# Layer 1's mixture of experts: every expert for every token, or the two chosen ones from a sorted list

## The chip, the cores and the metric

The kernel runs on one NeuronCore of a Trainium2 chip. The core has a matrix engine (TensorE, PE in the profile), a vector engine (VectorE, DVE), an activation engine (ScalarE, ACT), GpSimd (POOL) and a queue engine that issues transfers (SyncE, SP). PE writes its results to PSUM, eight banks of 128 partitions; the other data lie in SBUF or in DRAM. The metric is the device time of one execution in microseconds; lower is better. Float32 is used everywhere but in the attention scores, whose operands are split into bfloat16 parts.

## The reference

Four sequences of 1,024 tokens with 128 features (4,096 tokens, 32 tiles of 128) pass two layers. Each layer normalises x to xn, takes an attention s of xn and a gate g = silu(ffn(xn)), and returns x + s*g. In layer 1 the ffn is a mixture of eight experts with two chosen per token:

```python
logits = einsum('th,eh->te', x, router_w)
topk_logits, topk_idx = top_k(logits, 2)
probs = softmax(topk_logits)
combine = zeros((T, E)).at[arange(T)[:, None], topk_idx].add(probs)
hmid = gelu(einsum('th,efh->etf', x, w1) + b1[:, None, :])      # F = 256
y = einsum('etf,ehf->eth', hmid, w2) + b2[:, None, :]
out = einsum('eth,te->th', y, combine)
```

Written so, all eight experts are computed for every token and six of the eight results are multiplied by zero. Layer 1's attention is causal and differential, with 8 pairs of heads.

## The kernel before

The program has four blocks, one after the other, each with its own instruction lists for the five engines: the token stage of layer 0, its attention stage, the token stage of layer 1 and its attention stage.

**The token stage** (`token_stage(layer, ...)`) goes over 8 groups of 512 tokens. `steps` interleaves three things in the order of the expert number k = 0..7: the experts of group g (`body("expert")`), the front of group g+1 (transposes, router logits, projections q, k, v, the choice of experts, the split of q and k into three bfloat16 parts), and the statistics and normalisation of group g+2. In layer 1 `hidden` does two matmuls of 512 columns per expert (L866), ACT applies gelu with the bias (L800), eight matmuls of 128 columns give the expert's result (L898; each float32 matmul stands in the trace as two), and DVE adds it, weighted by the column C of the routing matrix, to the accumulator ACC (L1084). The bias b2 comes in by a small matmul of C (L940). ACT and DVE turn ACC into G, half of the silu by tanh, and SP stores it in `g_dram` (L750).

The split of q and k: DVE clamps them into FQ (L983), ACT rounds to PARTS (L831), GpSimd forms the rest (L682), ACT rounds that (L847), GpSimd forms the third part (L685). SP stores each group with one issue for v (L728), six for q (L736) and three for k (L745). PARTS has two buffers.

**The attention stage** (`attention_stage`) goes over 32 units of 128 queries. Its order on each engine is fixed ahead by `attention_plan`, which places tasks by costs and aims (`COST`, `AIM`). The tasks of a unit that matter here: GpSimd splits the row maxima (`msplit`, L1321 to L1327) and SP copies them in six small transfers next to the queries (L1266), on which PE's exponent scores wait; PE turns the output back (`oback`), DVE divides (`onorm`), GpSimd finds the root mean square by Newton steps (`orms`, L1331 to L1334), PE turns and projects (`oturn` L1467, `oproj` L1470), DVE multiplies by the gate (`final`, L1564), GpSimd adds x (L1341) and SP stores. After that addition GpSimd loads x and g for the unit two further on (`load_xg`, L1303 and L1304).

x of layer 1's first groups is loaded near the end of the attention stage of layer 0, into the buffer KR that layer 1 does not need (`X1`, `XN1`), and DVE normalises the first group there, in the task `final` of the last unit (L512).

## Time and profile before

| What | Value |
|---|---|
| Time, median of 3 runs | 1991.66 us (1989.51 to 1996.56) |
| Span of the profiled execution, whose page gives no other time | 1994.7 us |
| PE busy | 1724.8 us, 86% of the span |
| DVE / ACT / POOL busy | 1335.0 / 1194.0 / 1128.4 us |
| Instructions | 78,600 |

The busy time is that of the whole span; the four blocks differ, so the table by stretch in the rows below says more. The profiled span lies 3.0 us above the median of the runs and inside their range.

### The profile page before, as it was taken

How to read it: one execution, taken by the hardware profiler on the slowest of the kernel's cores; microseconds unless marked ns; L12 is line 12 of the kernel's file. 1: busy time of each engine (PE TensorE's matmuls, PEld its weight loads, DVE VectorE, ACT ScalarE, POOL GpSimd, SP SyncE). 2: the span in 40 equal slices, each digit the busy share in tenths (PEclk: the TensorE clock that was granted, in tenths of full speed). 3: DMA queues.
4: the chain of work that ended last, by engine and by line, in shares of the span. 5: the costliest groups of instructions: out<-in, count | busy, mean ns of one | idle time of the engine just before them, and what ended most of it. 6: DMA issues, size and time to landing. Idle time of an engine off the chain costs nothing. (4 is left out here: it accounts for less than half of the span.)

```text
span 1994.7 us, 78600 instructions
## 1 busy us (share of the span) xinstructions
PE 1724.8 (86%) x34080; PEld 1310.1 (66%) x34080; DVE 1335.0 (67%) x1975; ACT 1194.0 (60%) x1438; POOL 1128.4 (57%) x1489
## 2 busy tenths in 40 slices
PE   6887789999999989999988689999967878788886
PEld 4666678777787777778766566667635555555554
DVE  5552777777777758877776244544477888777882
ACT  2333477777787768777876534444425656566565
POOL 4755589987899769987995522221012333334333
PEclk9988799999998999999998789999958999999898
DMA  3476032222322222222112122133112112121100
GB/s 111 124 212 173 24 96 76 76 71 76 88 69 80 62 76 83 86 70 70 48 59 69 58 68 82 58 91 97 54 26 50 31 49 48 37 59 31 26 24 17
DMA packets 166301, 139.91 MB, mean 70 GB/s; under 512 B 91715, under 2 KB 157014, under 8 KB 160454
## 3 DMA queue, kind: packets, MB, share of 16 engines
q1 hardware_dynamic: 150966, 100.40, 17.2%
q10 hardware_dynamic: 9616, 21.89, 4.5%
q0 software_dynamic: 5376, 12.59, 2.2%
q8 instruction: 271, 4.44, 0.9%
q14 instruction: 72, 0.59, 0.1%
HBM read 90.91 MB, written 43.12 MB: 67 GB/s over the span
## 5 line engine op out<-in xcount | busy, mean ns | idle before, releaser
L1364 ACT ACTIVATE a_EX<-bank 128x1024 f32<-128x1024 f32 x624 | 615.4, 1026 | 288.9 <-PE bank L1236 235.0
L1490 DVE TENSOR_TENSOR a_PM<-bank,a_PM 128x1024 f32<-128x1024 f32 x336 | 401.7, 1221 | 129.2 <-PE bank L1236 118.0
L1316 POOL TENSOR_TENSOR a_SN<-a_SN,a_MB 128x1024 f32<-128x1024 f32 x176 | 421.0, 2429 | 48.0 <-DMA a_MB<-m_dram 47.2
L1513 DVE TENSOR_REDUCE a_M<-bank 128x2 f32<-128x1024 f32 (+3 forms) x304 | 339.0, 1163 | 82.0 <-PE bank L1249 53.3
L1453 PE MATMUL bank<-a_EX,VV 128*32 128x128 f32 x9984 | 359.7, 288 | 6.5 <-issue 4.9
L1236 PE MATMUL bank<-QS,KS 51*128 51x128 bf16 (+1 forms) x4992 | 234.9, 228 | 93.9 <-DMA QS<-a_MP 29.9
L1453 PEld LDWEIGHTS bank<-a_EX,VV 128*32 128x32 f32 x9984 | 269.8, 114 | 51.0 <-issue 22.7
L1236 PEld LDWEIGHTS bank<-QS,KS 51*128 51x128 bf16 (+1 forms) x4992 | 156.7, 99 | 185.8 <-issue 52.0
L1360 ACT ACTIVATE a_SN<-bank 128x1024 f32<-128x1024 f32 x176 | 176.7, 1024 | 57.6 <-PE bank L1215 56.3
L1368 ACT ACTIVATE a_SN<-a_SN 128x1024 f32<-128x1024 f32 x176 | 184.9, 1060 | 34.7 <-POOL a_SN L1316 34.7
L1215 PE MATMUL bank<-QP,rel_t 112*128 112x32 bf16 x5632 | 197.9, 177 | 3.0 <-issue 2.7
L1215 PEld LDWEIGHTS bank<-QP,rel_t 112*128 112x128 bf16 x5632 | 170.3, 96 | 4.0 <-issue 3.9
L1084 DVE SCALAR_TENSOR_TENSOR t_ACC<-bank,t_C,t_ACC 128x128 f32<-128x128 f32 x256 | 72.0, 344 | 145.9 <-PE bank L898 144.7
L898 PEld LDWEIGHTS bank<-t_w,t_HM 128*128 128x128 f32 x1024 | 123.8, 194 | 49.2 <-ACT t_HM L800 31.3
L1236 PE MATMUL bank<-QS,KR 48*128 48x128 bf16 (+1 forms) x2688 | 124.0, 224 | 29.9 <-DVE a_PM L1490 12.8
L1210 PE MATMUL bank<-QN,KS 112*128 112x64 bf16 x2816 | 141.5, 193 | 8.6 <-PEq L671 7.6
L1249 PE MATMUL bank<-KS,QS 48*128 48x128 bf16 (+3 forms) x1152 | 117.8, 293 | 28.6 <-DVE a_M L1513 14.7
L898 PE MATMUL bank<-t_w,t_HM 128*128 128x128 f32 x1024 | 128.8, 280 | 10.9 <-ACT t_HM L800 9.5
L529 POOL COPY QP<-QS 48x1024 bf16<-48x1024 bf16 x64 | 138.1, 2157 | 0.0
L1236 PEld LDWEIGHTS bank<-QS,KR 48*128 48x128 bf16 (+1 forms) x2688 | 79.4, 97 | 75.1 <-issue 28.9
L866 PE MATMUL bank<-t_XT,t_w 128*128 128x512 f32 x256 | 124.3, 609 | 0.0
L1497 DVE TENSOR_TENSOR a_PM<-a_SN 128x1024 f32<-128x1024 f32 x64 | 97.8, 1527 | 33.5 <-ACT a_SN L1360 27.6
(163 smaller groups left out, 2410.2 us busy)
## 6 DMA issues: line engine op xcount, KB each, us to landing
a_MB<-m_dram SPq DMA_DIRECT2D x32, 1024.0 KB, 5.0
QS<-q_dram SPq DMA_DIRECT2D x192, 96.0 KB, 2.9
KS<-k_dram ACTq DMA_DIRECT2D x16, 768.0 KB
q_dram<-t_PARTS SPq DMA_DIRECT2D x32, 192.0 KB, 2.8
k_dram<-t_PARTS SPq DMA_DIRECT2D x16, 384.0 KB, 2.9
QS<-a_MP SPq DMA_DIRECT2D x384, 2.0 KB
KR<-kr_dram ACTq DMA_DIRECT2D x8, 576.0 KB
q_dram<-t_PARTS SPq DMA_DIRECT2D x32, 128.0 KB, 2.6
```

Of the source, the lines that this page charges most:

```text
L529: last = pool.tensor_copy(QP[rows, r, :, :, a], QS[rows, q, :, :, :].rearrange("k p h (q b) -> k q (p h) b", b=2)[:, :, :, a])
L898: last = pe.matmul(y, HM[:, k % 2, h, t * P:(t + 1) * P], w2[:, k, h, :], start=h == 0, stop=h == 1)
L1210: pe.matmul(out_b[:, :, 4 * pair:4 * pair + 4], KS[0:KD, it.u // NB % 2, pair, it.jb * P:(it.jb + 1) * P], QN[:, r, pair, q0:q0 + CQ // 2, ...
L1215: last = pe.matmul(out_b[:, i, :], rel_t[:, y:y + P], QP[:, r, q0 + i, :, :].rearrange("k h a -> k (h a)"), start=False, stop=i == CQ // 2 ...
L1236: last = pe.matmul(bank[:, 2 * it.n + hh, k * P:(k + 1) * P], kblock(hh, rows, it.u, it.jb, pair), QS[hh * HALF:hh * HALF + rows, it.u % Q ...
L1316: pool.tensor_tensor(near_view(sn), near_view(sn), as_near(MB[:, :, :], it.part), ALU.add)\
L1360: act.activation(near_buffer(u, jb)[:, part, :], src.rearrange("p b c -> p (b c)"), ACT.Copy).then_inc(act_done, 1)
L1364: act.activation(as_banks(EX[:, it.need % ER[layer]], part), by_head, ACT.Exp, scale=SCALE).then_inc(act_done, 1)
L1368: act.activation(sn, sn, ACT.Exp, scale=SCALE).then_inc(nexp_done, 1)
L1453: last = pe.matmul(dst_o, VV[:, u // NB % 2, jb, vo:vo + 32], ex, start=bool(it.first) and h < 4, stop=bool(it.last), skip_group_check=True)
L1490: dve.tensor_tensor(pm, mb.rearrange("p hh (k i) -> p hh k i", k=4), pm, ALU.max).then_inc(max_used, 1)
L1513: dve.tensor_reduce(target.rearrange("p (hh k) -> p hh k", hh=2)[:, :, p0:p0 + g], mb[:, :, 0:g * width].rearrange("p hh (k j) -> p hh k j ...
```

## The change

Layer 1's token stage becomes a function of its own, `routed_stage`, with two halves (chunks) of 16 tiles, 4 groups each. Each half is normalised whole and its logits are taken first. `route` picks two experts per token and works out, with three matmuls and some small DVE operations, a place for each (token, choice) pair in a list sorted by expert, each expert's part padded to tiles of 128: 39 tiles ("steps") per half. GpSimd scatters the normalised rows to these places in DRAM (`xs_dram`) by 32 indirect transfers per half. The list is read back in quads of four steps, turned by PE, run through the step's expert, whose number is read into a register of each engine, and stored in `y_dram`. The q, k and v work of a half comes after its routing; all of it comes before the first step. The third part of the split moves from GpSimd to DVE.

The gate is no longer stored. In layer 1's attention stage GpSimd gathers, per unit, the two result rows of each token by indirect transfers, weights and adds them (`mix`), ACT takes a tanh, and GpSimd forms twice the silu (`gate`). The plan's costs and order are as before. In layer 0's attention stage SP also writes zeros over both lists (26 transfers of 192 KB), and the first half's x, not its first group, is loaded, measured and normalised near the end. Unchanged: layer 0's token stage, the attention of both layers.

```diff
+CHUNKS = 2
+CT = T // P // CHUNKS
+CG = GROUPS // CHUNKS
+STEPS = (2 * CT * P + E * (P - 1)) // P
+QUADS = -(-STEPS // 4)
+XGR = 4
...
+        def routed_stage(stage):
...
+            FQ = local("FQ", [P, 2, 2, GROUP])
+            FR = local("FR", [P, 2, 2, GROUP])
+            PARTS = local("PARTS", [P, 2, 3, 2, GROUP], BF16)
...
+            W = local("W", [P, 4, FF])
+            XS = local("XS", [P, 3, 4, P])
+            XST = local("XST", [P, 2, 4, P])
+            HM = local("HM", [P, 3, 2, P])
+            Y = local("Y", [P, 3, 4, P])
...
+                def _(pool):
+                    pool.memset(VA[:, :, :, :, VD:VD + 1], 1.0).then_inc(v_ones, 1)
+                    pool.wait_ge(zeroed, 16 * (CHUNKS * STEPS // 3))
+                    for c in range(CHUNKS):
+                        pool.wait_ge(slots_ready, c + 1)
+                        for t in range(CT):
+                            for k in range(2):
+                                at = SLOT[:, k, c * CT + t:c * CT + t + 1]
+                                pool.indirect_dma_start(out=xs_dram[c], out_offset=bass.IndirectOffsetOnAxis(ap=at, axis=0),
+                                                        in_=X1[c][:, t, :], in_offset=None).then_inc(scattered[c], 16)
...
+                    def load_slots(q):
+                        c, i = divmod(q, QUADS)
+                        sp.wait_ge(scattered[c], 16 * 2 * CT)
+                        if q >= 3:
+                            sp.wait_ge(xs_psum, q - 2)
+                        size = quad_size(q)
+                        sp.dma_start(XS[:, q % 3, 0:size, :], xs_dram[c].rearrange("(s p) d -> p s d", p=P)[:, 4 * i:4 * i + size, :])\
+                          .then_inc(xs_in[q % 3], 16)
+
+                    def store_y(q):
+                        c, i = divmod(q, QUADS)
+                        size = quad_size(q)
+                        sp.wait_ge(y_ready, steps_before(q) + size)
+                        sp.dma_start(y_dram[c].rearrange("(s p) d -> p s d", p=P)[:, 4 * i:4 * i + size, :], Y[:, q % 3, 0:size, :])\
+                          .then_inc(y_out[q % 3], 16)
...
+                    for f in range(GROUPS):
+                        store_v(f)
+                        store_qk(f)
+                        if f == 5:
+                            for q in range(3):
+                                load_slots(q)
+                    for u in range(QR):
+                        load_q(1, sp, u)
+                    for q in range(CHUNKS * QUADS):
+                        store_y(q)
+                        if q + 3 < CHUNKS * QUADS:
+                            load_slots(q + 3)
...
+                    def first_part(f):
+                        if f >= 2:
+                            act.wait_ge(qk_stored[f % 2], QKS * (f // 2))
+                        act.wait_ge(qk_taken, 2 * f + 2)
+                        act.activation(PARTS[:, f % 2, 0, :, :], FQ[:, f % 2, :, :], ACT.Copy).then_inc(p1_ready, 1)
...
+                    for f in range(CG, GROUPS):
+                        values(f)
+                        first_part(f)
+                        if f > CG:
+                            second_part(f - 1)
+                    second_part(GROUPS - 1)
...
+                    turn_slots(0)
+                    for c in range(CHUNKS):
+                        pe.wait_ge(steps_ready, c + 1)
+                        for i in range(QUADS):
+                            q = c * QUADS + i
+                            if q + 1 < CHUNKS * QUADS:
+                                turn_slots(q + 1)
+                            for k, e in enumerate(experts_of(mybir.EngineType.PE, c, i)):
+                                s = step_index(c, 4 * i + k)
+                                hidden(q, k, s)
+                                if len(behind) == 2:
+                                    result(*behind.pop(0))
+                                behind.append((q, k, s, e))
...
+                    dve.wait_ge(route_in, 16 * len(loads))
+                    route(0)
+                    for f in range(CG):
+                        take(f)
+                        if f:
+                            third_part(f - 1)
+                        second_rest(f)
+                    third_part(CG - 1)
+                    dve.drain()
+                    chunk_statistics(dve, 1)
+                    dve.drain()
+                    rsqrt(dve, rstd1[:, :], var1[:, :], newton1[:, :], fused=True)
+                    chunk_normalise(dve, 1)
+                    dve.drain()
+                    route(1)
...
+                            for k, e in enumerate(experts_of(mybir.EngineType.DVE, c, i)):
+                                s = step_index(c, 4 * i + k)
+                                weights(s, e)
+                                if len(behind) == 3:
+                                    add_bias(*behind.pop(0))
+                                behind.append((q, k, s, e))
...
+                        for k in range(2):
+                            pool.indirect_dma_start(out=XG[:, r, 1 + k, :], out_offset=None, in_=y_dram[tile // CT],
+                                                    in_offset=bass.IndirectOffsetOnAxis(ap=SLOT[:, k, tile:tile + 1], axis=0))\
+                                .then_inc(xg_in[r], 16)
+                        pool.dma_start(XG[:, r, 0, :], x_v[tile]).then_inc(xg_in[r], 16)
+
+                    def mix(u):
+
+                        r, tile = u % XGR, row_of(u)
+                        pool.wait_ge(xg_in[r], 48 * (u // XGR + 1))
+                        pool.tensor_scalar(XG[:, r, 1, :], XG[:, r, 1, :], PW[:, 0, tile:tile + 1], None, ALU.mult)
+                        pool.tensor_scalar(XG[:, r, 2, :], XG[:, r, 2, :], PW[:, 1, tile:tile + 1], None, ALU.mult)
+                        pool.drain()
+                        pool.tensor_tensor(XG[:, r, 1, :], XG[:, r, 1, :], XG[:, r, 2, :], ALU.add).then_inc(z_ready, 1)
+
+                    def gate(u):
+
+                        r = u % XGR
+                        pool.wait_ge(th_ready, u + 1)
+                        pool.tensor_tensor(XG[:, r, 2, :], TH[:, u % 2, :], XG[:, r, 1, :], ALU.mult)
+                        pool.drain()
+                        pool.tensor_tensor(XG[:, r, 1, :], XG[:, r, 1, :], XG[:, r, 2, :], ALU.add).then_inc(gate_ready, 1)
...
+                    for u in range(2 if layer == 0 else XGR):
+                        load_xg(u)
...
+                            if layer == 1:
+                                if u + 1 < UNITS:
+                                    gate(u + 1)
+                                if u + XGR < UNITS:
+                                    load_xg(u + XGR)
+                                if u + 2 < UNITS:
+                                    mix(u + 2)
...
+                            if layer == 1 and 1 <= u < UNITS - 1:
+                                tanh(u + 1)
```

The step functions that the loops call: `turn_slots` turns a quad's tiles with four PE transposes; `hidden` does two 128-column matmuls with weights that DVE copied (`weights`, 256 columns per step) and `result` two more with w2 picked by the register; `add_bias` is one DVE addition of 128 columns from PSUM; `take`, `second_rest` and `third_part` are DVE's clamp and two subtractions of 1,024 columns per group.

## Rows read from the trace of the kernel before

**Rows 1.** Busy time by stretch: PE PEld DVE ACT POOL, clock, DMA, GB/s

```profile
1141.80:1444.50 302.70, 285.17 (x1568) 201.15 (x1568) 138.17 (x523) 120.20 (x193) 57.06 (x114) 0.96 0.26 78
1444.50:1994.70 550.20, 439.62 (x8832) 287.66 (x8832) 406.71 (x556) 316.52 (x385) 196.17 (x704) 0.90 0.16 37
```

**Rows 2.** Timeline, one expert of layer 1 (start, length, engine, line)

```profile
1424.31 1.88 PE L866 MATMUL bank<-t_XT,t_w 128*128 128x512 f32 x4
...
1426.03 1.95 PE L898 MATMUL bank<-t_w,t_HM 128*128 128x128 f32 x16
...
1427.81 1.88 PE L866 MATMUL bank<-t_XT,t_w 128*128 128x512 f32 x4
```

**Rows 3.** Groups by line, 1130:1470 (count, busy, mean ns, idle)

```profile
L1084 DVE SCALAR_TENSOR_TENSOR t_ACC<-bank,t_C,t_ACC 128x128 f32<-128x128 f32 x256 | 72.0, 344 | 145.9 <-PE bank L898 144.7 <-issue 0.6
...
L983 DVE TENSOR_SCALAR t_FQ<-bank 128x512 f32<-128x512 f32 x16 | 10.9, 682 | 4.4 <-PE bank L918 2.7 <-PE bank L910 1.7
...
L831 ACT ACTIVATE t_PARTS<-t_FQ 128x1024 bf16<-128x1024 f32 x8 | 8.5, 1057 | 27.1 <-DVEq L986 27.1
...
L1010 DVE COPY t_LG<-bank 128x32 f32<-128x32 f32 x8 | 1.5, 191 | 1.1
...
L1364 ACT ACT_TABLE_LOAD x1 | 1.3, 1283 | 0.1
```

**Rows 4.** The page's costliest groups: a DVE operation over 1,024 columns

```profile
L1490 DVE TENSOR_TENSOR a_PM<-bank,a_PM 128x1024 f32<-128x1024 f32 x336 | 401.7, 1221 | 129.2 <-PE bank L1236 118.0
```

**Rows 5.** Timeline, SP: the stores of one group's q and k

```profile
1415.04 3.92 SPq L736 DMA_DIRECT2D q_dram<-t_PARTS  x6
...
1419.32 1.55 SPq L745 DMA_DIRECT2D k_dram<-t_PARTS  x3
```

**Rows 6.** DMA issues, 1141 to 1445: KB, us to landing

```profile
k_dram<-t_PARTS SPq DMA_DIRECT2D x8, 384.0 KB, 2.9
...
KR<-x_mid POOLq DMA_DIRECT2D x6, 256.0 KB, 3.2
```

**Rows 7.** Timeline, DVE: statistics and normalisation of four tiles

```profile
1115.94 0.88 DVE L496 BATCH_NORM_STATS2 stats<-KR 128x6 f32<-128x128 f32 x4
...
1137.11 1.11 DVE L512 TENSOR_SCALAR KR<-KR,mv,rstd 128x128 f32<-128x128 f32 x4
```

**Rows 8.** Busy time by stretch: PE with gaps, and its granted clock

```profile
100.00:110.00 10.00, 6.82 (x42) 6.16 (x42) 4.45 (x10) 3.99 (x6) 6.03 (x11) 0.83 0.91 284
...
1455.00:1460.00 5.00, 2.64 (x10) 0.52 (x10) 5.00 (x5) 0.00 (x0) 0.00 (x0) 0.50 0.01 1
```

**Rows 9.** Waits of POOL, 1470 to 1970 us: total, times, longest

```profile
POOL a_XO L1341 <- DVEq L1566: 112.0, 30, 13.7
POOL a_SS L1331 <- DVEq L1549: 85.4, 24, 7.4
```

**Rows 10.** Timeline, attention of layer 1: POOL, and PE behind it

```profile
1615.61 0.42 POOL L1323 TENSOR_TENSOR a_MS<-a_MR,a_MP 16x128 f32<-16x128 f32 x1 [3.25 <-issue]
...
1647.28 0.19 POOL L1331 TENSOR_SCALAR a_SS<-a_SS 128x8 f32<-128x8 f32 x1 [7.37 <-DVEq L1549]
...
1652.30 0.40 POOL L1334 TENSOR_TENSOR a_OF<-a_OD,a_RS 128x128 f32<-128x128 f32 x1
...
1654.45 0.33 PE L1467 MATMUL bank<-eye,a_OF 128*128 128x128 f32 x1
...
1660.45 0.54 POOL L1304 DMA_DIRECT2D a_XG<-g_dram  x1
...
1662.29 0.19 POOL L1331 TENSOR_SCALAR a_SS<-a_SS 128x8 f32<-128x8 f32 x1 [1.29 <-DVEq L1549]
...
1758.27 0.19 POOL L1331 TENSOR_SCALAR a_SS<-a_SS 128x8 f32<-128x8 f32 x1 [2.56 <-DVEq L1549]
```

**Rows 11.** Timeline, layer 1's first unit: POOL's split, PE's first exponents

```profile
1451.11 0.42 POOL L1327 TENSOR_TENSOR a_MP<-a_MS,a_MP 16x128 bf16<-16x128 f32 x1
...
1465.63 0.61 PE L1236 MATMUL bank<-QS,KS 51*128 51x128 bf16 x8
```

More of the change, by code:

```diff
@@ L51, with routing_tables @@
 NR = 2
+CHUNKS = 2
[4 more added lines that the diff above has]
+XGR = 4
+def routing_tables():
+    k = np.arange(P)
+    t, e = k // E, k % E
+    below = (k[:, None] < k[None]).astype(np.float32)
+    before = ((e[:, None] == e[None]) & (t[:, None] < t[None])).astype(np.float32)
+    same = (e[:, None] == np.arange(E)[None]).astype(np.float32)
+    lower = np.tile((np.arange(E)[None] < np.arange(E)[:, None]).astype(np.float32).reshape(1, E * E), (P, 1))
+    rows = np.tile((P * np.arange(CT)).astype(np.float32)[None], (P, 1))
+    steps = np.tile(np.arange(4 * QUADS).astype(np.float32)[None], (P, 1))
+    return np.concatenate([below, before, np.ones((P, P), np.float32), same, lower, rows, steps], 1)
+ROUTE = 3 * P + E + E * E + CT + 4 * QUADS
 def position_table_rows(rel):
@@ L719, in _ @@
                     parts(GROUPS - 1)
-                    if layer == 0:
-                        for u in range(NR):
-                            permute(pool, u)
+                    for u in range(NR):
+                        permute(pool, u)
                 @block.sync
@@ L876, in body @@
                     def body(kind, f, p, k):
-                        if kind == "expert" and layer == 0:
+                        if kind == "expert":
                             if k == 0 and f == 0:
@@ L925, in body @@
                             last.then_inc(proj_psum, 1)
-                        if kind == "front" and k == 4 and f == 0 and layer == 1:
-                            pe.wait_ge(expert_in, 16 * len(expert_loads))
-                            hidden(0, 0, 0)
                         if kind == "front" and k == 5:
@@ L1293, in _ @@
                     for r in range(2):
[L1294 removed]
+                        sp.wait_ge(stored[r], STORED1 * (layer + 1))
                 @block.gpsimd
@@ L1327, in _ @@
                             pool.tensor_tensor(mp[:, 2], MS[:, :], mp[:, 1], ALU.subtract).then_inc(m_split, 1)
+                            if layer == 1 and u == 1:
+                                mix(0)
+                                mix(1)
                         elif it.kind == "orms":
```

824 lines of the change are left out of this document (552 added, 272 removed).

## The prediction

> **What bounds the kernel now.** I began with busy time by stretch, cut where the blocks begin and end. Layer 1's token stage takes 302.7 us, PE is busy for 285.2 of them (94%) and no other engine for half; the attention behind it takes 550.2 us with PE at 80%, DVE at 74% and POOL at 36% [rows 1]. So PE sets the token stage. Its timeline shows the cadence: one expert of one group every 3.50 us (1424.31 to 1427.81), of which the sixteen short matmuls take 1.95 and four long ones the rest [rows 2]. 64 such turns make 224 us. DVE's additions are mostly waits for PE [rows 3]. The attention stage was read by POOL's waits, since the change gives POOL work there: 112.0 us before the addition of x and 85.4 before `orms`, some 6.6 us in a unit of 16 [rows 9].
>
> **What goes.** All 64 turns, 224 us of PE. The list has 78 steps. A step is four float32 matmuls of 128 columns, eight records; sixteen records take 1.95 us [rows 2], 1.78 when run on into their followers, so a step is 0.9 us of PE and a quad with its four transposes 4.1 to 4.2. Twenty quads are 82 us: PE loses about 140 us of work. That would be the gain if PE still set the end. I expect it doesn't.
>
> **The first half's front.** Transposes and logits of 16 tiles take PE about 10 us from a cold start. `route` is 27 small DVE operations in a row. One over 32 columns takes 0.191 us, one over 512 takes 0.682 [rows 3], so 128 columns take 0.29, with the drain between them 0.36: 9.7 us. Three rounds through PE, with `project(0)` queued ahead of them, add some 4.5. The first `take` is at 24 us.
>
> **The groups.** `take` is 2 x 0.69, `first_part` 1.06 [rows 3], `second_rest` and `third_part` 1.22 each (a DVE operation with two inputs over 1,024 columns [rows 4]). Unhindered that is 6.2 us a group. But ACT's order is `first_part(f+2)`, then `second_part(f+1)`; `first_part(f+2)` waits until group f is stored, and `parts_ready(f+1)` needs `second_part(f+1)`. So stores and splits take turns: SP issues q in 3.9 and k in 1.6 us [rows 5], landing takes 2.9 [rows 6], and then 1.06 + 1.06 + 1.22 and handovers, 3.5 us: 12 us a group where two buffers seem to promise 6. From the first `take` of a half to its last part I get 8.7 + 24 + 3.7 = 36.4 us. The first half ends at 60.4.
>
> **Between the halves.** DVE alone measures and normalises 16 tiles: 4 x 0.88 and the aggregates (under half of that), 2.4 for the Newton steps, 4 x 1.11 [rows 7], together 12.4. Last group's turn and logits 3.4, routing 12.5: `take(4)` at 88.7, the second half ends at 125.1. DVE's step loop begins there. The 32 scatters of a half lie beside this unless one costs POOL over 3 us. SP is late: it still has to store two groups (to 133) and issue eight q loads (5.2), so `load_slots(3)` goes out at 139 and PE has quad 3 at 142, when the first quads are done.
>
> **The steps.** What limits a quad is none of the engines. XS has three buffers, and SP issues `load_slots(q+3)` only behind `store_y(q)`, whose last result comes two steps into quad q+1. PE turns quad q+3 before it starts quad q+2. From the result of step 4q+3: handover and `add_bias` 0.45 (0.34 with both inputs [rows 3]), two issues of 0.4 each, landing of 256 KB 3.2 [rows 6]: 4.5 us. Then PE has 0.5 of transposes and 1.8 of two steps before the next such result. Period P = 6.9 at full clock. PE would then be busy 60%, in bursts. The rows at either level: a stretch with PE busy 68% had a granted clock of 0.83, one with half-busy PE 0.50, its level of 1.2 GHz [rows 8]; at the lower level the 2.4 us of PE double and P is 9.3. The registers' reads have no row; below, nothing (PE's sequencer does them while it waits), above, one vector operation's 0.19 for each of four [rows 3]. I take P = 8.0, with half of each. Sixteen periods from 142 are 270, the last seven steps and the block's change 14: 284 us against 302.7, **-19**. A break-even P is 9.2.
>
> The Trainium skill ("DMA: Bandwidth & Descriptors", Latency and other measured facts) puts a register load at about 600 ns at the least. No row here shows one. If four stood in PE's path, P would be 2.4 larger and the stage 38 us longer than my sum, still the same story with a dearer step.
>
> **Layer 0's attention.** Normalising 16 tiles where four stood takes 4.4 us where 1.11 was [rows 7], at the tail that the last unit waits for: **+3.3**. The 26 writes of zeros cost SP 0.4 each behind a store; SP has room, so +1, at most 10.
>
> **Layer 1's attention.** Start: POOL issues four units' gathers before its first split. At 3.8 us each that is 15 where 2.2 was, with the wake the split ends at 1464 instead of 1451.5; six issues and landing take 6, PE reaches the exponents at 1465.6 [rows 11]. **+2** on a part where most is hidden.
>
> Each unit: POOL loses one issue (0.54 [rows 10]) and gets two gathers, `mix` (two of 0.3, an addition of 0.45, drains: 1.4) and `gate` (1.2). A gather has no row. Below it costs like a plain load, 0.54; above, by the split that started right after two loads and sat 3.25 us waiting for nothing shown [rows 10], 2.2 for one load with its unseen part. I take 1.2, and 0.5 for the unseen part of the load behind them: A = 5.0 us more per unit, bounds 3.3 and 6.3. All of it stands between the addition of unit u and `orms` or the next split. The idle time there in eight consecutive units is 7.4, 1.3, 1.9, 1.3, 0, 7.3, 0 and 2.6 (first and last in [rows 10]), and after `orms` PE comes 0 to 1.6 us later (1652.70 to 1654.45 is the longest). So PE stalls 0, 2.4, 2.3, 3.7, 5.0, 0, 5.0, 1.4: 19.8 us in eight units. PE idles a fifth of this block anyway and finds full queues after a stall, so I take 60%: 12 per eight units, 45 in all. POOL's own loop says the same: 6.6 us idle less 5.0 leaves it the tightest engine. Bounds 12 (A = 3.3) and 85. **+45.**
>
> Sum: -19 + 3.3 + 1 + 2 + 45 = +32. The profiled 1994.7 would become 2027; against the median of 1991.7 that is **2024 us**.
>
> **Rivals.** *The short list wins* (faster): P = 7 because PE keeps 2.4 GHz and landing is nearer the 2.9 us, and POOL's additions cost 12: -35 + 4 + 2 + 12 = -17, 1975. For it speaks that POOL waits 6.6 us a unit; against, that this waiting is not at the place where the work is put. It decides when A is below about 3.5 and P below 7.3. 0.24. *Nothing left over*: P near 7 with +30 in the attention, 1992, within 6 us. 0.08. *The steps crawl*: lower clock and reads in the path, P = 10.4, stage +20: 2063. For it: the half-busy row at 0.50 [rows 8]. Against: at 1.2 GHz PE would be 79% busy (8.2 of 10.4), and the stretch at 68% already had 0.83. 0.20. *Table loads*: `tanh` now stands among the exponentials; if each unit made ACT reload twice, 64 x 1.28 us [rows 3] = 82 on an engine that is 58% busy, 30 to 60 of it seen: 2070. 0.03. The trace has exp's load once at the start of this block, and no tanh behind it. The Trainium skill ("ScalarE: Activation LUTs", Table sets) lists tanh in exp's set, by which no load is added; that is why this is small. My forecast, slower by 0.5 to 3%, has 0.45.
>
> **The numbers.** A difference under 0.3% (6 us) can't be told from none here. Faster takes the first rival, 0.24; same 0.08; slower the rest, 0.68. The likeliest case by itself is 2002 to 2052. The range 1972 to 2085 takes in the first rival's centre and the crawling steps, with A = 6.3.
>
> **What would show it.** Right: PE's busy time in the new stage under 160 us while the stage still takes 265 to 305; waits of PE for XS in each quad; parts ready every 12 us; `orms` starting right after `mix` with POOL busy through each unit, and `oturn` on PE waiting for it. Wrong: a stage near 220 us (the chain through SP is not the limit, or splits overlap stores), or an attention block still at 550 us (then the gathers are cheap or PE's slack is larger than I read), or ACT table loads in each unit.

## The result: slower by 4%, in the direction forecast and nearly three times the size

| | Time (median) | Ratio to the kernel before |
|---|---|---|
| Before, beside it | 1992.4 us | 1 |
| Changed kernel | 2082.7 us (2068.0 to 2099.4) | 1.0418 [1.0375, 1.0461] |
| Changed kernel, measured again beside the experiments | 2087.8 us (2080.1 to 2095.6) | 1.0448 [1.0404, 1.0493] |
| Forecast | 2024 us (1972 to 2085) | 1.016 |

The direction is the one forecast and the time lies at the upper end of the range. The profile shown here is that of the second measurement, because the first one, 2099.4 us, fell into a slower execution. Its span is 2093.7 us, 99.0 above the span of before. Busy time by stretch, cut where the blocks begin and end (columns: stretch, length, busy us and records of PE, PEld, DVE, ACT, POOL, granted clock, DMA share, GB/s):

```profile
0.00:1155.50 1155.50, 1001.59 (x23680) 824.02 (x23681) 789.17 (x924) 758.58 (x860) 885.66 (x672) 0.94 0.31 88
1155.50:1466.30 310.80, 170.18 (x910) 145.90 (x910) 105.34 (x329) 75.92 (x191) 68.68 (x65) 0.72 0.40 116
1466.30:2093.70 627.40, 464.89 (x8832) 305.23 (x8832) 410.46 (x557) 324.42 (x417) 325.69 (x896) 0.84 0.16 35
```

The cut behind the token stage is DVE's last addition; PE's first matmul of the attention, at which [rows 1] is cut, comes 1.4 us later, so that by the cut of [rows 1] the stage is 1.4 us longer than shown here and the attention as much shorter. Against [rows 1] PE lost 115 us of work in layer 1's token stage (285.2 to 170.2), and the stage is 8 us longer all the same: PE is busy for 55% of it, and the granted clock fell from 0.96 to 0.72. The attention behind it, in which PE's program is the same, takes 627.4 us where 550.2 were, PE's records there are 25 us longer in sum, and the clock fell from 0.90 to 0.84. Layer 0's part before both ends 13.7 us later.

| Term | Forecast | Measured |
|---|---|---|
| Layer 0's attention: 16 tiles at the end, zero writes | +4.3 | +13.7 |
| Layer 1's token stage | -19 | +8.1 |
| Layer 1's attention, until the first unit is stored | +2 | -5 |
| Layer 1's attention, the units | +45 | +82 |
| Sum | +32 | +99 |

The last two are read from SP's stores of the output: the first came 55.7 us after the block's start before and 50.6 now, and from there to the store of the 29th unit it is 460.6 and 541.7 us; the rest of the 82 is behind it. The terms are read from one profiled execution of each kernel, 99.0 us apart; the medians are 90 us apart.

**The steps.** The timeline of all engines over one quad in the middle of the stage (start, length, engine, line, and in brackets the idle time before it with what ended it):

```profile
1390.25 0.36 SPq L1173 DMA_DIRECT2D y_dram<-t_Y  x1
1390.71 0.43 SPq L1166 DMA_DIRECT2D t_XS<-xs_dram  x1
...
1393.69 0.66 PE L1312 MATMUL bank<-eye,t_XS 128*128 128x128 f32 x4 [1.37 <-DMA t_XS<-xs_dram]
...
1395.36 0.68 PE L1321 MATMUL bank<-t_XST,t_W 128*128 128x128 f32 x4 [1.00 <-issue]
...
1397.53 0.29 DVE L1468 TENSOR_TENSOR t_Y<-bank,t_b 128x128 f32<-128x128 f32 x1 [0.40 <-PE bank L1330]
1397.85 0.36 SPq L1173 DMA_DIRECT2D y_dram<-t_Y  x1
```

This is the chain of the forecast, link by link: SP stores the results (L1173), only then issues the load of the quad three further on (L1166), PE waits for it and turns it 3.0 us later (L1312), and the result on which SP's next store waits (L1468) is there at 1397.53. The stores follow each other at 1390.25 and 1397.85, 7.6 us apart at a granted clock of 0.94; to the next store it is 9.5 us, at 0.69. From 1321.71 to 1458.00 there are 16 quads, 8.5 us each. In them PE waits 26.6 us for the loads of XS by name and 3.2 more ahead of one quad's transposes, 1.9 a quad, and 15.0 us ahead of first steps, 0.9 a quad; its records take the other 5.7. One more stretch of waiting is in SP's own timeline, just ahead of the load of quad 3:

```profile
1278.46 4.40 SPq L1152 DMA_DIRECT2D q_dram<-t_PARTS  x6
...
1285.93 18.01 SPq L1152 DMA_DIRECT2D q_dram<-t_PARTS  x6
...
1312.33 0.45 SPq L1166 DMA_DIRECT2D t_XS<-xs_dram  x1
```

The six issues of the last group's q took 18.0 us where the seventh group's took 4.4 and a group of before 3.9 [rows 5]. 13.9 of the 18.0 us pass between its first issue and its second. So the load of quad 3 went out 156.8 us after the start of the stage; 139 were forecast. In the 7.5 us before this group's issue the 16 transfer engines were busy for all of it (DMA share 1.01), and in the 13.9 us for about half (0.53), and ACT issues its loads of the first keys and values for the attention at 1279.7 to 1281.0. What held the queue is not shown.

**The units.** GpSimd (POOL) and PE in one unit of layer 1's attention:

```profile
1911.97 0.46 POOL L1778 TENSOR_TENSOR a_XO<-a_XO,a_XG 128x128 f32<-128x128 f32 x1 [4.14 <-DVEq L2028]
...
1913.85 1.07 POOL L1710 DMA_INDIRECT a_XG<-y_dram,KR  x1 [0.41 <-issue]
1915.22 1.00 POOL L1710 DMA_INDIRECT a_XG<-y_dram,KR  x1 [0.30 <-issue]
...
1920.52 0.46 POOL L1722 TENSOR_TENSOR a_XG<-a_XG 128x128 f32<-128x128 f32 x1 [2.45 <-issue]
...
1922.83 0.20 POOL L1762 TENSOR_SCALAR a_SS<-a_SS 128x8 f32<-128x8 f32 x1
...
1927.71 0.40 POOL L1765 TENSOR_TENSOR a_OF<-a_OD,a_RS 128x128 f32<-128x128 f32 x1
...
1928.26 0.45 PE L1921 MATMUL bank<-eye,a_OF 128*128 128x128 f32 x1 [6.80 <-POOL a_OF L1765]
```

From the addition of x (L1778) to the end of `mix` (L1722) GpSimd waits for no other engine. A split of row maxima and the root mean square (L1762 to L1765) follow without a gap, and PE's `oturn` (L1921) has stood idle for 6.8 us when it comes. The waits in the 28 units between the first store and the last show where such time went (us in total, times, longest); first the kernel before:

```profile
PE bank L1467 <- POOL a_OF L1334: 8.1, 9, 2.4
...
POOL a_XO L1341 <- DVEq L1566: 96.0, 28, 10.7
POOL a_SS L1331 <- DVEq L1549: 78.6, 22, 7.4
POOL a_XG L1303 <- issue: 16.5, 29, 0.6
...
POOL a_MS L1323 <- issue: 14.2, 7, 3.3
```

and then the changed one:

```profile
PE bank L1921 <- POOL a_OF L1765: 66.3, 21, 10.5
...
POOL a_XO L1778 <- DVEq L2028: 96.4, 27, 10.5
POOL a_XG L1722 <- issue: 43.7, 28, 9.1
POOL a_XG L1710 <- issue: 20.2, 56, 0.4
POOL a_SS L1762 <- DVEq L2003: 14.2, 7, 2.7
```

PE waits 58 us more for the root mean square. GpSimd's wait ahead of it gave way (78.6 to 14.2), its wait ahead of the addition of x did not move at all (96.0 to 96.4). The busy time of the same 28 units, before and changed:

```profile
1501.00:1961.00 460.00, 384.73 (x7939) 253.26 (x7931) 358.35 (x493) 286.33 (x349) 173.86 (x622) 0.94 0.18 39
```

```profile
1517.00:2059.00 542.00, 409.81 (x7921) 271.56 (x7917) 361.60 (x490) 292.56 (x375) 287.92 (x791) 0.86 0.17 37
```

PE's records grew by 25.1 us at a clock of 0.86 in place of 0.94, its busy share fell from 84% to 76%, and its idle time grew by 56.9 us (75.3 to 132.2). 25 and 57 are the whole 82. PE's waits for everything but the root mean square stayed as they were, 62.9 and 62.8 us. GpSimd got 114.1 us of work. Its time without its waits for DVE and ACT grew from 281.0 to 431.4 us, which takes in the waits for nothing that the profile names: 150.4 in 28 units, 5.4 a unit.

### The profile page after: what moved, and what is told of

The parts are those of the page before. It is cut to its first block and busy times, and to the rows that moved or that the text cites. A ratio compares the mean times of both kernels' runs of the same rounds, so it can differ in the third digit from the quotient of the medians.

```text
span 2097.6 us, 78405 instructions
## 1 busy us (share of the span) xinstructions
PE 1644.0 (78%) x33422; PEld 1280.9 (61%) x33422; DVE 1304.7 (62%) x1809; ACT 1157.3 (55%) x1468; POOL 1269.5 (61%) x1632
## 5 line engine op out<-in xcount | busy, mean ns | idle before, releaser
L1944 DVE TENSOR_TENSOR a_PM<-bank,a_PM 128x1024 f32<-128x1024 f32 x336 | 401.1, 1221 | 143.4 <-PE bank L1627 132.2
L1907 PE MATMUL bank<-a_EX,VV 128*32 128x128 f32 x9984 | 378.3, 294 | 6.9 <-issue 5.0
L1907 PEld LDWEIGHTS bank<-a_EX,VV 128*32 128x32 f32 x9984 | 280.4, 117 | 60.0 <-issue 30.5
L1627 PE MATMUL bank<-QS,KS 51*128 51x128 bf16 (+1 forms) x4992 | 240.1, 232 | 85.7 <-DMA QS<-a_MP 23.3
L1627 PEld LDWEIGHTS bank<-QS,KS 51*128 51x128 bf16 (+1 forms) x4992 | 162.4, 101 | 175.7 <-issue 53.1
L1809 ACT ACTIVATE a_SN<-bank 128x1024 f32<-128x1024 f32 x176 | 176.9, 1024 | 61.9 <-PE bank L1606 60.6
L1710 POOL DMA_INDIRECT a_XG<-y_dram,KR x64 | 64.4, 1007 | 202.4 <-issue 202.4
L1264 ACT ACTIVATE t_HM<-bank,t_b 128x128 f32<-128x128 f32 x156 | 48.7, 364 | 138.1 <-PE bank L1321 138.0
L1951 DVE TENSOR_TENSOR a_PM<-a_SN 128x1024 f32<-128x1024 f32 x64 | 99.0, 1547 | 34.2 <-ACT a_SN L1809 27.9
L1601 PEld LDWEIGHTS bank<-QN,KS 112*128 112x128 bf16 x2816 | 106.5, 98 | 15.1 <-issue 12.5
L1136 POOL DMA_INDIRECT xs_dram<-KR x64 | 68.9, 1076 | 73.1 <-DVE KR L1426 42.5
```

The source lines that it names most:

```text
L1601: pe.matmul(out_b[:, :, 4 * pair:4 * pair + 4], KS[0:KD, it.u // NB % 2, pair, it.jb * P:(it.jb + 1) * P], QN[:, r, pair, q0:q0 + CQ // 2, ...
L1627: last = pe.matmul(bank[:, 2 * it.n + hh, k * P:(k + 1) * P], kblock(hh, rows, it.u, it.jb, pair), QS[hh * HALF:hh * HALF + rows, it.u % Q ...
L1809: act.activation(near_buffer(u, jb)[:, part, :], src.rearrange("p b c -> p (b c)"), ACT.Copy).then_inc(act_done, 1)
L1907: last = pe.matmul(dst_o, VV[:, u // NB % 2, jb, vo:vo + 32], ex, start=bool(it.first) and h < 4, stop=bool(it.last), skip_group_check=True)
L1944: dve.tensor_tensor(pm, mb.rearrange("p hh (k i) -> p hh k i", k=4), pm, ALU.max).then_inc(max_used, 1)
```

## The experiments

Ratios are to the kernel before, in runs on the same chip; beside them the start of layer 1's token stage, its length, and what follows, of the one profiled execution.

| Run | Ratio [95%] | Start | Stage | Attention |
|---|---|---|---|---|
| changed kernel again | 1.0448 [1.0404, 1.0493] | 1155.5 | 310.8 | 627.4 |
| list loads first | 1.0225 [1.0201, 1.0249] | 1149.8 | 264.6 | 625.1 |
| second part first | 1.0315 [1.0276, 1.0353] | 1159.0 | 292.4 | 623.9 |
| no register reads, list loads first | 1.0078 [1.0058, 1.0098] | 1158.6 | 235.3 | 625.1 |
| zeros in stage | 1.0460 [1.0427, 1.0493] | 1148.2 | 318.0 | 627.6 |
| no gate work | 1.0103 [1.0070, 1.0136] | 1159.2 | 307.7 | 564.5 |
| plain loads | 1.0300 [1.0240, 1.0361] | 1155.2 | 307.0 | 591.5 |
| gate behind the root mean square | 1.0486 [1.0432, 1.0540] | 1153.5 | 309.3 | 626.9 |
| mix on DVE | 1.0415 [1.0367, 1.0463] | 1153.5 | 305.2 | 616.2 |
| gate ahead of the addition | 1.0176 [1.0127, 1.0225] | 1149.5 | 305.9 | 578.3 |
| three edits | 1.0195 [1.0136, 1.0255] | 1150.1 | 254.4 | 625.8 |
| three edits, moved | 1.0118 [1.0064, 1.0171] | 1154.0 | 257.7 | 608.1 |
| shared out | 1.0044 [1.0020, 1.0067] | 1148.9 | 258.2 | 596.1 |
| stage and place | 0.9836 [0.9806, 0.9867] | 1152.3 | 247.8 | 560.7 |

### The changed kernel again

> The changed kernel once more, as the measure for the runs beside it. Both theories: 2065 to 2085 us, a ratio of 1.036 to 1.046 to the kernel before. If its profile is undisturbed, the two blocks of layer 1 should show where the 83 us come from: by the theory that the attention lost most, the block of the steps takes 310 to 322 us and the attention 605 to 620 us.

The control for all below. The stage came out as expected, the attention 7 us above.

### List loads first

```diff
 for q in range(CHUNKS * QUADS):
-    store_y(q)
     if q + 3 < CHUNKS * QUADS:
         load_slots(q + 3)
+    store_y(q)
```

> SP issues the load of quad q+3 ahead of the store of quad q; nothing else differs. Theory A (the chain result, store, load, landing, transposes sets the 9.1 us of a quad): the load is then a quad early, its landing is hidden, the quad falls to what PE needs, 5.3 us at full clock (4.2 of work and 1.1 of register reads) or 9.3 at 1.2 GHz; PE being busier raises the clock, so some 6 us, and the stage gains 16 x 3 = 40 to 50 us. Rival B (the granted clock and the register reads set it, the chain only comes out level with them): the quad stays above 8.3 us and the gain is under 15 us.

Two lines changed places and the stage lost 46 us. The same quads in the timeline of this kernel, and below them the busy time of 15 quads:

```profile
1344.23 0.36 SPq L1173 DMA_DIRECT2D y_dram<-t_Y  x1
...
1344.69 0.45 SPq L1166 DMA_DIRECT2D t_XS<-xs_dram  x1
...
1345.47 0.49 PE L1312 MATMUL bank<-eye,t_XS 128*128 128x128 f32 x3
1347.34 0.68 PE L1321 MATMUL bank<-t_XST,t_W 128*128 128x128 f32 x4 [1.37 <-DVE t_W L1454]
```

```profile
1315.50:1399.60 84.10, 64.88 (x535) 61.50 (x534) 38.10 (x135) 37.18 (x118) 0.00 (x0) 0.99 0.34 93
```

and the changed kernel's 16 quads:

```profile
1321.70:1458.00 136.30, 91.55 (x568) 84.34 (x568) 40.60 (x143) 39.68 (x126) 0.00 (x0) 0.83 0.22 61
```

The transposes no longer wait for the load, a quad takes 5.6 us in place of 8.5, and PE, busy for 77% and not 67%, has a clock of 0.99 in place of 0.83. Of the 2.9 us, 1.9 are the wait for the load and 1.4 are PE's shorter records (5.7 to 4.3 a quad); the wait ahead of a quad's first step, the one that remains, grew by 0.3. Theory A stands. The edit touches SP's order alone and the clock rose with it, so the low clock came with the waiting.

### No register reads

The expert of each step is `(4 * q + k) % E`, a constant, so that the wrong weights are used; list loads first is kept.

```diff
-_, values = nc.values_load_multi_w_load_instructions(step_e[0:1, c, 4 * q:4 * q + size], engines=[engine], ...)
+values = [(4 * q + k) % E for k in range(size)]
```

> List loads first, and the expert of each step is a constant of the program (step number modulo 8) in place of one read into a register on PE, ACT and DVE, so the wrong expert's weights are used. Against list loads first alone (ratio 1.0225, 5.5 us a quad). Theory A (four reads hold PE 1.0 to 1.2 us at the head of each quad, before its first step): a quad takes 4.3 to 4.7 us, 15 to 22 us less in the stage, a ratio near 1.013. Rival B (the reads lie beside a wait for XST or W that comes as late without them): under 5 us.

SP's loads of the list then follow each other like this:

```profile
1340.10 0.45 SPq L1165 DMA_DIRECT2D t_XS<-xs_dram  x1
1344.24 0.45 SPq L1165 DMA_DIRECT2D t_XS<-xs_dram  x1
```

4.14 us a quad against 5.60: what stands at the head of a quad for its four expert numbers cost 1.46 us, and the stage 29 us, more than the 15 to 22 expected. The forecast had bounded it by 0 and 0.76. PE is now busy for all of the 15 quads from 1323.02 to 1384.20, at a clock of 1.00. What the 1.46 us consist of is in the records of line 1122 of list loads first, shortest, median and longest duration in ns:

```profile
L1122 DVEq FUSED_REGOPS  x78: 183/190/203, 1277.6 to 1407.8; - x78
...
L1122 DVEq TENSOR_LOAD <-t_step_e x20: 344/653/1304, 1276.8 to 1405.9; - x20
```

By their names, and since the kernel states bounds for the number (`min_val=0, max_val=E - 1`), they check it; that is read from the names and not tested. So most of the time on DVE's queue goes to what follows the load; no run leaves out that part alone. The Trainium skill ("DMA: Bandwidth & Descriptors", Latency and other measured facts) has about 600 ns as the least for a register load. The median of this trace lies near it, but the shortest load of four numbers took 0.34 us on DVE and 0.33 on PE, and the measurement decides. The 2.4 us that the forecast worked out for four loads do not apply, since one load brings the four.

### Second part first

```diff
 values(f)
-first_part(f)
 second_part(f - 1)
+first_part(f)
```

> ACT rounds the second part of group f-1 before the first part of group f, which waits for the store of group f-2; nothing else differs. Theory A (stores and splits take turns, 12.3 us a group, because the second part of f-1 is queued behind that wait): a group takes what SP needs for q and k and the landing of the store before, 6.5 to 9 us, and the stage gains 6 x 3.5 to 5.5, some 20 to 33 us. Rival B (the transfers themselves or SP's issues set the group): under 8 us gained, and the parts still come 11 us or more apart.

In the changed kernel the third parts (DVE L1448), which end a group, and ACT's first and second parts stand so:

```profile
1195.54 1.06 ACT L1213 ACTIVATE t_PARTS<-t_FQ 128x1024 bf16<-128x1024 f32 x1 [9.32 <-DMA k_dram<-t_PARTS]
1196.50 1.04 ACT L1217 ACTIVATE t_PARTS<-t_FR 128x1024 bf16<-128x1024 f32 x1
...
1197.58 1.22 DVE L1448 TENSOR_TENSOR t_PARTS<-t_FR,t_PARTS 128x1024 bf16<-128x1024 f32 x1 [8.66 <-ACT t_PARTS L1217]
...
1209.92 1.23 DVE L1448 TENSOR_TENSOR t_PARTS<-t_FR,t_PARTS 128x1024 bf16<-128x1024 f32 x1 [8.79 <-ACT t_PARTS L1217]
```

12.3 us from one to the next, ACT's first part waiting for the k store of two groups ago and the second part queued behind it. With the two lines exchanged:

```profile
1202.07 1.27 DVE L1448 TENSOR_TENSOR t_PARTS<-t_FR,t_PARTS 128x1024 bf16<-128x1024 f32 x1
1210.45 1.27 DVE L1448 TENSOR_TENSOR t_PARTS<-t_FR,t_PARTS 128x1024 bf16<-128x1024 f32 x1 [1.12 <-ACT t_PARTS L1217]
```

8.4 us. The stage lost 18 us in the profile, a little less than the 20 to 33 expected, and the kernel 27 in the timed runs (1.0448 to 1.0315). Theory A stands.

### Zeros in the stage

The 26 writes in layer 0's attention become six of 832 KB on SP at the head of the new stage.

```diff
+for c in range(CHUNKS):
+    for i in range(3):
+        sp.dma_start(xs_dram[c].rearrange("(s p) d -> p s d", p=P)[:, 13 * i:13 * i + 13, :],
+                     bv[:, None, :].broadcast_to([P, 13, D])).then_inc(zeroed, 16)
 sp.wait_ge(v_ones, 1)
```

> The zeros over both lists are written in six transfers of 832 KB at the start of layer 1's token stage, in place of 26 of 192 KB during layer 0's attention. Theory A (the 26 transfers cost layer 0's attention some 8 us, most of it where the traces part between 440 and 525 us): the start of layer 1's stage comes back from 1151 to 1159 us to 1144 to 1149 us and the kernel gains 5 to 10 us, as the stage itself has time for them before its first scatter is needed. Rival B (the difference there is the tail of normalisation and scatter between executions): no more than 4 us gained, stage start still beyond 1150 us.

The stage starts earlier in this profile, as theory A has it, but it is 7 us longer and nothing is gained in the whole (1.0460 against 1.0448), where 5 to 10 us were expected. Fourteen profiles of kernels with the zero writes in place start the stage between 1148.9 and 1159.2 us, 1153.6 on average, with no other difference in layer 0's part; before, it was 1141.8. The 1148.2 us of this run lie only 0.7 below that spread, so that the zero writes are what moved the start is not shown. 2.3 of them are the end that the forecast priced: from PE's last operation of layer 0 to its first of layer 1 it is 5.9 us in place of 3.6.

### No gate work

No mix, tanh and gate; one plain tile of the result list is loaded and used as the gate.

```diff
-for k in range(2):
-    pool.indirect_dma_start(out=XG[:, r, 1 + k, :], ...)
+pool.dma_start(XG[:, r, 1, :], y_dram[tile // CT][(tile % CT) * P:(tile % CT + 1) * P, :]).then_inc(xg_in[r], 16)
...
-gate(u + 1)
-mix(u + 2)
...
-tanh(u + 1)
```

> Leaves out the weighting of the two expert results: layer 1's attention loads x and one plain tile of the result list per unit, as many transfers as before the change, and does no mix, no tanh and no gate. Theory A (the added work on GpSimd is what the attention lost): the attention block falls back to 550 to 556 us and the kernel by 60 to 70 us, to 2010 to 2020. Rival B (part of the loss has another cause, such as the later start, the deeper load queue or a lower clock): it falls by less than 40 us.

62.9 us of the 77 come back, and 69 in the timed runs (1.0448 to 1.0103). PE's wait for the root mean square in the 28 units is

```profile
PE bank L1905 <- POOL a_OF L1760: 14.0, 8, 3.3
```

Theory A stands for four fifths of the loss in the attention. 13 us stay in the units of this run; what holds them was not isolated.

### Plain loads

```diff
 for k in range(2):
-    pool.indirect_dma_start(out=XG[:, r, 1 + k, :], ...)
+    pool.dma_start(XG[:, r, 1 + k, :], y_dram[tile // CT][(tile % CT) * P:(tile % CT + 1) * P, :]).then_inc(xg_in[r], 16)
```

> Replaces the two gathers of a unit by two plain loads of one tile of the result list (other rows are weighted and added; mix, tanh and gate stay). Theory A (a gather costs GpSimd more than a plain load, about 1.3 us against 0.57 with its gap, and makes the drain behind it wait): GpSimd loses 1.5 to 2.5 us of its added 6.7 a unit and the attention gains 12 to 30 us. Rival B (the arithmetic on GpSimd and its place are all that counts): under 8 us.

The attention gains 36 us in the profile, more than theory A had, and the kernel 30 in the timed runs (1.0448 to 1.0300). A gather's record is 1.007 us against 0.601 for the plain load of x beside it:

```profile
L1710 POOL DMA_INDIRECT a_XG<-y_dram,KR x64 | 64.4, 1007 | 192.4 <-issue 192.4
L1713 POOL DMA_DIRECT2D a_XG<-x_mid x32 | 19.2, 601 | 0.1
```

With its gap of 0.30 a gather costs about 1.3 us, close to the 1.2 that the forecast took without a row. Two gathers are thus 1.4 us a unit dearer than two loads, and 1.1 us a unit of it came back on the whole. The other half of theory A fell: GpSimd's wait ahead of the addition in `mix`, behind the drain, is as long with plain loads as with gathers (43.7 us there):

```profile
POOL a_XG L1720 <- issue: 42.3, 28, 9.0
```

### The same work in three places

Behind the root mean square (the block that stood behind the addition goes, and this takes its place):

```diff
 elif it.kind == "orms":
     ...
-    if u == 0:
-        gate(0)
+    if layer == 1:
+        gate(u)
+        if u and u + 3 < UNITS:
+            load_xg(u + 3)
+        if u + 2 < UNITS:
+            mix(u + 2)
```

> GpSimd does gate, the gathers and mix of each unit behind the root mean square of that unit and not ahead of it; the work is the same. Theory A (it hurts because it stands ahead of the operation that PE waits for, while GpSimd idles 3 us a unit before its addition of x): the attention gains 20 to 40 us of its 75. Rival B (GpSimd is full, so its place does not matter, or the row maxima queued behind it now come late): under 10 us gained, or a loss.

Theory A fell, and rival B had named the reason. PE's wait for the root mean square fell to 2.2 us and another took its place:

```profile
PE bank L1627 <- DMA QS<-a_MP: 63.7, 9, 12.6
```

Where GpSimd's split of the row maxima stands behind `orms` in the order, it is the one that comes late now; SP copies those rows, and PE's exponents wait for them. The third place is behind both:

```diff
 elif it.kind == "final":
+    if layer == 1:
+        if u and u + 3 < UNITS:
+            load_xg(u + 3)
+        if u + 2 < UNITS:
+            mix(u + 2)
     pool.wait_ge(scaled, u + 1)
     ...
-    if layer == 1:
-        if u + 1 < UNITS:
-            gate(u + 1)
-        if u + XGR < UNITS:
-            load_xg(u + XGR)
-        if u + 2 < UNITS:
-            mix(u + 2)
+    if layer == 1 and u + 1 < UNITS:
+        gate(u + 1)
```

> The gathers and mix of a unit stand ahead of GpSimd's addition of x, which waits 96 us in 28 units for DVE, so behind both the root mean square and the row maxima; gate stays behind the addition. The work is the same. Theory A (3.4 us of that wait a unit take up half of the added work, the rest is pushed into the next unit): the attention gains 25 to 45 us. Rival B (PE's next order of work is bound to all three, so it makes no difference where the work stands, as behind the root mean square): under 10 us.

The attention fell from 627.4 to 578.3 us with every operation kept, and the kernel by 54 us in the timed runs, more than the 25 to 45 of theory A. GpSimd's waits in the 28 units:

```profile
POOL a_SS L1762 <- DVEq L2003: 71.7, 24, 5.2
...
POOL a_XG L1722 <- issue: 20.8, 28, 1.6
...
POOL a_XO L1783 <- DVEq L2028: 8.5, 6, 4.8
```

The work now fills the wait ahead of the addition of x (96.4 to 8.5), and GpSimd again waits for the root mean square's input (71.7) and not PE for its output, which is no longer among PE's eight longest waits. The clock is back at 0.93, though PE's records are still 13 us longer than before (398.1 and 384.7), so that not all of the 25 us above can be put down to the clock with certainty:

```profile
1507.00:1999.00 492.00, 398.08 (x7959) 260.82 (x7949) 362.75 (x493) 291.58 (x377) 284.84 (x789) 0.93 0.18 40
```

### Sparing GpSimd

In the first of these DVE does `mix` and `gate`, and GpSimd keeps its place of loading; the second adds the two edits of the stage and loads behind the root mean square; the third loads ahead of the addition of x; in the fourth ACT multiplies by the weights, GpSimd adds, DVE gates. DVE's part in the first three, and what replaces `mix` on ACT in the fourth:

```diff
+dve.tensor_scalar(XG[:, r, 1, :], XG[:, r, 1, :], PW[:, 0, tile:tile + 1], None, ALU.mult)
+dve.drain()
+dve.scalar_tensor_tensor(XG[:, r, 1, :], XG[:, r, 2, :], PW[:, 1, tile:tile + 1], XG[:, r, 1, :], ALU.mult, ALU.add)
...
+dve.scalar_tensor_tensor(XG[:, r, 1, :], TH[:, u % 2, :], 1.0, XG[:, r, 1, :], ALU.add, ALU.mult)
```

```diff
+for k in range(2):
+    last = act.activation(XG[:, r, 1 + k, :], XG[:, r, 1 + k, :], ACT.Copy, scale=PW[:, k, tile:tile + 1])
```

> DVE does mix and gate (a multiplication and two fused operations of 128 columns a unit), GpSimd keeps the gathers. GpSimd loses 3.8 us a unit and its waits between the operations, DVE gets about 1.2 us. Theory A (GpSimd's time sets the pitch of a unit): the attention gains 35 to 55 us, since only 2 us of gathers a unit stay. Rival B (the gathers and their unseen part hold GpSimd, not the arithmetic; or DVE at 65% becomes the one waited for): under 20 us gained.

> List loads first, second part first and mix and gate on DVE together, and the gathers of a unit behind its root mean square. If the parts add up: 46 + 26 + 40 to 55 us less than the 2085 of the changed kernel, 1958 to 1973 us, a ratio of 0.980 to 0.988: the kernel before is beaten. Rival B (the parts overlap, PE's lower clock or SP's queue taking back what each gives): 1985 us or more.

> As the three edits together (list loads first, second part first, mix and gate on DVE), but with the gathers of a unit ahead of GpSimd's addition of x and not between the root mean square and the row maxima. Theory A: the wait of PE for the rows of the maxima, 31 us there, goes, and the kernel comes to 1990 to 2005 us, level with the one before. Rival B (DVE is the one waited for by now): above 2015 us.

> The two stage edits, and the gate's work shared out: ACT multiplies the two rows by their weights, GpSimd gathers and adds them ahead of its addition of x, DVE does the gate in one fused operation. GpSimd then has 3.4 us more a unit than before the change, ACT 0.9, DVE 0.4. Theory A (each engine waited for by PE has to be spared): the attention at 575 to 590 us, the kernel at 1975 to 1992 us, below the one before by up to 1%. Rival B (the longer chain of handovers between the three engines stalls one of them): 2000 us or more.

With `mix` and `gate` on DVE, the attention gained 11 us where 35 to 55 were expected. Less was taken from GpSimd than the 3.8 us a unit of the expectation: its time without waits for DVE and ACT fell by 66 us in the 28 units, 2.4 a unit (431.4 to 365.3), since part of the unnamed wait behind the gathers only moved to its next operations (28.5 us ahead of the split of the row maxima, 19.5 where 4.4 were in the root mean square). PE's wait for the root mean square went from 66.3 to 27.9 us, but DVE is itself waited for, and two of PE's waits for it grew from 20.1 and 8.9 us to

```profile
PE bank L1627 <- DVE a_M L1955: 25.6, 47, 1.3
PE bank L1640 <- DVE a_M L1955: 20.5, 28, 1.6
```

so that part of the loss only changed its place. The three edits together came out on rival B's side, for the reason that the kernel with the work behind the root mean square had shown: loads behind the root mean square make the row maxima late (31.4 us of waits). Moved, they gave 1.0118, shared out 1.0044, and both came out on rival B's side: PE's two waits for DVE take 32.5 and 19.5 us in the first and 28.3 and 14.8 in the second. Each has less work on GpSimd than the kernel in which it was only moved, and each is slower in the attention (608.1 and 596.1 against 578.3, or against 560.7 in the kernel below, which has the edits of the stage as they do).

### Stage and place

List loads first, second part first, and the move ahead of the addition; nothing is shared out.

> List loads first, second part first, and the gathers and mix ahead of the addition of x, all on GpSimd; no work is shared out. Theory A (the three losses are separate waits, so their cures add): 46 + 26 + 54 us less than 2087, 1955 to 1970 us, a ratio of 0.979 to 0.987, the kernel before beaten by some 30 us. Rival B (they overlap, as the three edits with DVE fell short): 1985 us or more.

1963.9 us, 1.6% below the kernel before and 5.9% below the changed one. The three parts add: their ratios lie 44, 27 and 54 us below that of the changed kernel, 125 in sum, and the whole lies 122 below. The stage takes 247.8 us where the dense one took 302.7, the attention 560.7 where it was 550.2. The sum holds for the whole and not block by block: the same attention program took 578.3 us in the profile of the move alone, and what makes the 17.6 us was not looked into.

## Why the forecast was too small

The direction was right. Two terms were mis-sized, by 27 us in the token stage and 37 in the units; the second holds the step that failed.

**What bounds the kernel now:** right for both blocks.

**The list and its steps:** PE's work in the stage fell by 115 us, and 140 were forecast from a quad of 4.1 to 4.2 us; the quad without register reads has 4.14. So the forecast's sign "PE's busy time in the new stage under 160 us" did not come (170.2). The same 910 records take 145.7 us in list loads first, 139.5 less than before, where the waiting is gone; so the rest is in PE's records at the lower clock.

**The first half and the groups:** right. The groups are 12.3 us apart (12 forecast), for the reason given, as the exchange of two lines shows. DVE's second half ended 126.4 us after the start (125.1 forecast).

**The steps' chain through SP:** right as a mechanism, shown by the exchange of store and load. Its size was off in two terms. The period is 8.5 us, not 8.0. That is a slip in the forecast's own sum: 6.9, half of the lower clock's 2.4 and half of the reads' 0.76 make 8.5, and 8.0 was written. The parts came out otherwise than forecast, so that the agreement with 8.5 is partly luck: the wait ahead of a quad's first step is 0.9 us, above its bound of 0.76, and PE's records are 1.6 us a quad longer than at full clock (5.7 against 4.1), while the load comes sooner (3.4 us from SP's store to the transposes in the quad above, 4.0 forecast). And the chain began 18 us late, 14 of them by the issue of the last group's q. 16 x 0.5 and 18 are 26 of the 27 us that the term was off. The forecast's "it still has to store two groups (to 133)" was priced by a group in a quiet stretch [rows 5]; SP had stored them at 150.7.

**Layer 0's attention:** +13.7 for +4.3. The end that was priced at 3.3 took 2.3; the start of the next stage varies by 10 us between the fourteen profiles, and the rest was not settled.

**The start of the attention:** the first exponents come 23.3 us after the start where it was 21.1, as forecast; the gathers, 12 us of them, lie beside DVE's maxima. The 5 us gained come behind that, where PE waited once for the copies of the row maxima, 8.3 us before and 1.1 now; the forecast had no term for it.

**The units:** the step that failed; +45 was forecast and +82 measured. GpSimd's added time was mis-sized a little: 5.4 us a unit, where the forecast took 5.0 and bounded it by 6.3. What failed is the discount on the stalls: "PE idles a fifth of this block anyway and finds full queues after a stall, so I take 60%". With 60% the list of eight units, 19.8 us, is 42 us in 28 units. PE's wait for the root mean square grew by 58 and its idle time in all by 57, while its other waits stayed at 63 us: no stall was made up from a fuller queue. The other and larger part is a term that the forecast put at nothing without a reason: PE's records took 25 us longer, at a clock of 0.86 in place of 0.94, as its busy share fell from 84% to 76%. The list without the discount, with 5.4 for 5.0, would give 2.8 us a unit or 78 us, near the 82 measured. That is luck: it has 20 us more of waiting than PE had, and nothing for the longer records. The sentence "this waiting is not at the place where the work is put" in the first rival was right: the 96 us ahead of the addition stayed as they were, and moving the work there gave 49 us of the attention.

**The table loads:** ACT's only table load in the attention block is

```profile
L1813 ACT ACT_TABLE_LOAD x1 | 1.3, 1283 | 0.1
```

as before. So the rival fell. The Trainium skill ("ScalarE: Activation LUTs", Table sets), which lists tanh in the set of exp, agrees with this trace.

## What to carry to other kernels

Work given to an engine that idles is only free at the place in its order where it idles: list its waits by place, ask which instruction of another engine stands behind each, and put the work ahead of the wait that nobody is behind. Here the attention lost 77, 77 or 28 us to the same instructions by their place alone, and taking them off the engine was worth less than moving them. In a queue that stores and prefetches, issue the prefetch first where its buffer is already free. And do not discount a stall of the engine that sets the end by its idle share; here it kept all 58 us of them and lost 25 more in longer records. Last, look at what a cost consists of: of the register reads here, what follows the load took longer than the load.

## What the runs showed of the hardware

- Four expert numbers in registers, with what goes with each, lengthened a quad by 1.46 us (5.60 against 4.14), with DVE and PE both reading ahead of a quad's first step. One load brought the four, 0.65 us in the median and 0.34 at the least on DVE; the two operations behind it took 0.28 us a number.
- Behind two gathers and a load, GpSimd's operation after the next drain waited 1.6 us on average and up to 9.1 us for nothing that the profile names (43.7 us in 28 units). With plain loads in place of the gathers it was as much (42.3 us, up to 9.0); where the same work stood ahead of the addition of x, it was 0.7 us and at most 1.6 (20.8 us).
- A gather of 128 rows of 512 bytes holds GpSimd for 1.0 us and a gap of 0.3; a plain load of the same 64 KB holds it for 0.54 to 0.60.
- PE's records took 409.8 us for the same 28 units that took 384.7 before: at a granted clock of 0.86 in place of 0.94. In the token stage PE at 67% busy had 0.83, at 77% 0.99.
